# Score matmuls of the first differential attention contract 32 rows instead of 64, and take the maps in another order

## What is computed

```python
def _L2_attn_ref(x, w_qkv, wo, lambda_q1, ..., norm_w):
    b, s, e, H, HD = 4, 512, 128, 16, 8
    q, k, v = to_heads(split(x @ w_qkv, 3))            # 16 heads of 8 dims
    q1, q2 = split(q, 2, axis=-1); k1, k2 = split(k, 2, axis=-1)   # 4 dims each
    a1 = softmax(einsum('bhsd,bhtd->bhst', q1, k1) * HD ** -0.5)
    a2 = softmax(einsum('bhsd,bhtd->bhst', q2, k2) * HD ** -0.5)
    a = a1 - lam * a2
    out = einsum('bhst,bhtd->bhsd', a, v)
    return (out / rms(out) * norm_w * 0.2) ... @ wo
```

## Time and profile before

| | us |
|---|---|
| median of three runs | 1867.42 |
| lowest and highest | 1865.07 and 1871.61 |
| the profiled execution's own time | 1868.42 |
| its span, first to last instruction | 1866.6 |
| the changed stage, kind 2, in the span | about 888 to 1294 |

### The profile page before, as it was taken

How to read it: one execution, slowest core, us unless ns; L and a number is a source line. 1 busy time by engine, 2 the same in 40 slices (tenths; PEclk the granted TensorE clock), 3 DMA queues, 4 the chain that set the end, 5 groups by cost and what they waited for, 6 DMA issues and landing times. The chain is left out here.

```text
span 1866.6 us, 27462 instructions
## 1 busy us (share of the span) xinstructions
PE 1517.4 (81%) x9043; PEld 824.1 (44%) x9102; DVE 1049.9 (56%) x2293; ACT 935.4 (50%) x2171; POOL 364.2 (20%) x507
## 2 busy tenths in 40 slices
PE   4895757999999686675599999997488795999879
PEld 4454643555555475674222222223378452223255
DVE  6577331333334525213788889895511576888656
ACT  3454334444444334112388788875222334888733
POOL 1230630000000162563130101000266101101000
PEclk7796877999999797788699999998698797999979
DMA  2002534020200444543330303000444304223000
GB/s 75 5 1 79 158 112 117 8 68 1 68 1 1 131 127 143 172 127 109 88 80 1 80 1 98 1 1 1 129 139 128 99 1 108 74 66 78 1 1 23
DMA packets 95893, 125.97 MB, mean 67 GB/s; under 512 B 14304, under 2 KB 65120, under 8 KB 95376
## 3 DMA queue, kind: packets, MB, share of 16 engines
q1 hardware_dynamic: 86096, 105.10, 19.7%
q0 software_dynamic: 7936, 16.27, 3.1%
q10 hardware_dynamic: 1728, 2.88, 0.8%
HBM read 87.41 MB, written 36.80 MB: 67 GB/s over the span
## 5 line engine op out<-in xcount | busy, mean ns | idle before, releaser
L2156 DVE TENSOR_REDUCE MAXI<-psum 128x2 f32<-128x1024 f32 x384 | 451.4, 1218 | 70.4 <-PE psum L1962 69.1
L2073 ACT ACTIVATE EX<-psum 128x512 f32<-128x512 f32 x768 | 408.2, 607 | 94.1 <-PE psum L1983 93.6
L2457 PE MATMUL psum<-EX,N 128*128 128x512 f32 x512 | 238.5, 609 | 0.0
L2519 ACT ACTIVATE EX<-psum 128x512 f32<-128x512 f32 x256 | 149.1, 599 | 174.2 <-PE psum L2449 174.2
L1983 PE MATMUL psum<-QM,KM 64*128 64x512 bf16 x768 | 219.8, 389 | 14.7 <-DVE REST L2147 5.0
L1962 PE MATMUL psum<-KM,QS 64*128 64x512 bf16 x768 | 175.1, 405 | 47.7 <-DVE MAXI L2156 22.6
L1993 PE MATMUL psum<-EX,VST 128*32 128x512 f32 x1536 | 205.4, 610 | 1.3 <-ACT OT L2087 1.3
L1191 PE MATMUL psum<-m_DOWN,m_H 128*128 x992 | 143.6, 292 | 35.5 <-DVE m_Y L1416 32.9
L1416 DVE TENSOR_SCALAR m_Y<-psum 128x128 f32<-128x128 f32 x124 | 35.8, 289 | 238.1 <-remote 129.3
L1177 PE MATMUL psum<-m_XT,m_W 128*128 128x128 f32 x992 | 151.9, 302 | 3.4 <-issue 3.4
L2570 DVE COPY OT<-psum 128x512 f32<-128x512 f32 x64 | 44.3, 692 | 187.0 <-PE psum L2457 187.0
(11 more groups left out here) (330 smaller groups left out, 2023.5 us busy)
## 6 DMA issues: line engine op xcount, KB each, us to landing
m_W<-in_w_dram SPq DMA_DIRECT2D x124, 256.0 KB
parts<-PART SPq DMA_DIRECT2D x24, 384.0 KB, 2.6
m_DOWN<-in_w_dram SPq DMA_DIRECT2D x32, 256.0 KB
parts<-PART SPq DMA_DIRECT2D x24, 256.0 KB, 2.5
rows<-N SPq DMA_DIRECT2D x16, 256.0 KB, 3.1
N<-y SPq DMA_DIRECT2D x16, 256.0 KB, 4.1
QS<-parts SPq DMA_DIRECT2D x32, 128.0 KB, 3.8
QS<-parts SPq DMA_DIRECT2D x16, 256.0 KB, 6.0
```

Source lines behind the costliest of these rows:

```text
L2073: act.activation(EX[:, n % 2, kt, MAPS[j], :], bank_of(("score", n, i)), ACT.Exp, scale=SM_SCALE).then_inc(S["exp"].sem, 1)
L2156: dve.tensor_reduce(MAXI[:, n % 2, qt, columns], pair(i), AX, ALU.max, negate=True).then_inc(S["reduced"].sem, 1)
L2457: last = pe.matmul(banks[4 + j], N[:, n // per_b * TB + kt, :], EX[:, n % 2, kt, j, :], start=kt == 0, stop=kt == TB - 1)
L2519: act.activation(EX[:, n % 2, kt, j, :], bank_of(("score", n, i)), ACT.Exp, scale=SM_SCALE, accum_out=SUMS[:, n % 2, j, kt:kt + 1]).then_i ...
```

## The change

A map's peak and score matmuls contract its own 32 partitions. `where` returns `slot * width` to `(slot + 1) * width`; `KM` loses its second copy and with it the clearing of 4 slots by VectorE and 4 by GpSimd and two semaphore waits of TensorE. The scores of kind 2 take the maps in the order 1, 3, 0, 2 (`SCORED`); the peak pairs keep theirs. Kind 3 has slots of 64 partitions and computes as it did. The diff, without the lines that only drop the copy's index from `where`'s result:

```diff
-        half_slots = slots // 2
-        KM = sb("KM", [P, buffers, 8, half_slots, L], BF16)
+        KM = sb("KM", [P, buffers, 8, L], BF16)
...
             slot = j % slots
-            rows = slice(slot // half_slots * 64, slot // half_slots * 64 + 64)
-            return rows, b % buffers, g * stacks + j // slots, slot % half_slots
+            return slice(slot * width, (slot + 1) * width), b % buffers, g * stacks + j // slots
 
         MAPS = {2: (0, 2, 1, 3), 3: (0, 1, 2, 3)}[kind]
+        SCORED = {2: (1, 3, 0, 2), 3: (0, 1, 2, 3)}[kind]
...
-                    if kind == 2 and i == 0 and n == 0:
-                        pe.wait_ge(zeroed.sem, zeroed.at(slots))
-                    if kind == 2 and i == 0 and n == per_b:
-                        pe.wait_ge(filled.sem, filled.at(2 + slots))
...
-                    r, buf, g, m = where(n, MAPS[at])
-                    pe.matmul(bank_of(("score", n, i)), KM[r, buf, g, m, kt * P:(kt + 1) * P],
-                              QM[r, n % 2, MAPS[at] // slots, :], start=True, stop=True).then_inc(S["score"].sem, 1)
+                    r, buf, g = where(n, SCORED[at])
+                    pe.matmul(bank_of(("score", n, i)), KM[r, buf, g, kt * P:(kt + 1) * P],
+                              QM[r, n % 2, SCORED[at] // slots, :], start=True, stop=True).then_inc(S["score"].sem, 1)
...
-                    act.activation(EX[:, n % 2, kt, MAPS[j], :], bank_of(("score", n, i)), ACT.Exp,
+                    act.activation(EX[:, n % 2, kt, SCORED[j], :], bank_of(("score", n, i)), ACT.Exp,
                                    scale=SM_SCALE).then_inc(S["exp"].sem, 1)
...
-                    for j in range(slots):
-                        dve.memset(KM[j * width:(j + 1) * width, 0, :, 1 - j % half_slots, :], 0.0
-                                   ).then_inc(zeroed.sem, 1)
...
-                    if kind == 2 and n < slots:
-                        pool.wait_ge(S["vstage"].sem, S["vstage"].at(n + 1))
-                        pool.memset(KM[n * width:(n + 1) * width, 1, :, 1 - n % half_slots, :], 0.0
-                                    ).then_inc(filled.sem, 1)
-                        pool.wait_ge(filled.sem, filled.at(3 + n))
```

More of the change, by code:

```diff
@@ L1823, in diff_attention @@
         filled = self.semaphore_of("da_filled")
-        zeroed = self.semaphore_of("da_zeroed")
         fixed = self.fixed
@@ L1919, in _ @@
                             to = slice(j * width, (j + 1) * width)
-                            for s, dst in ((0, QS[to, b % buffers, half, :]), (1, KM[to, b % buffers, half, j % half_slots, :])):
+                            for s, dst in ((0, QS[to, b % buffers, half, :]), (1, KM[to, b % buffers, half, :])):
                                 src = scratch[s, b].rearrange("c (d k g) t -> k (c d) g t", k=slots, g=8)[j, :, half, :]
@@ L1960, in peak @@
                     for k in range(2):
-                        r, buf, g, m = where(n, MAPS[2 * jp + k])
-                        last = pe.matmul(pair(i)[:, k, :], QS[r, buf, g, qt * P:(qt + 1) * P], KM[r, buf, g, m, :],
+                        r, buf, g = where(n, MAPS[2 * jp + k])
+                        last = pe.matmul(pair(i)[:, k, :], QS[r, buf, g, qt * P:(qt + 1) * P], KM[r, buf, g, :],
                                          start=True, stop=True)
@@ L1969, in place @@
                     out = bank_of(("place", n, s))
-                    _, buf, g, _ = where(n, s * slots)
+                    _, buf, g = where(n, s * slots)
                     pe.matmul(out, self.identb[:], QS[:, buf, g, :], start=True, stop=False)
@@ L2116, in _ @@
                         src = scratch[1, 0].rearrange("c (d k g) t -> k (c d) g t", k=slots, g=8)[j, :, half, :]
-                        act.dma_start(KM[to, 0, half, j % half_slots, :], src).then_inc(stacked[h].sem, 16)
+                        act.dma_start(KM[to, 0, half, :], src).then_inc(stacked[h].sem, 16)
                 for s in range(stacks):
@@ L2326, in diff_attention @@
         filled.passed(2)
-        if kind == 2:
-            zeroed.passed(slots)
-            filled.passed(slots)
         fixed.passed(32 * B)
```

## The result

| | before | changed |
|---|---|---|
| median of 5 runs, us | 1867.42 | 1884.03 |
| lowest and highest | 1864.67 to 1871.61 | 1878.03 to 1885.69 |
| the profiled execution's own time | 1868.42 | 1885.69 |
| mean granted clock of its span | 0.89 | 0.87 |

The ratio is 1.0083, with a 95% interval of 1.007 to 1.0096. The changed kernel is slower by 0.8%, 16.6 us, where 8.1 us less was forecast.

What follows compares the result with a forecast made beforehand. The stage was taken as bound by a loop through VectorE, ScalarE and TensorE, none full. Savings of 7.2 and 0.9, 8.1 us, took the profiled 1868.42 to 1860.3, or 1859.3 against the median; range 1850 to 1868.

Steps and rivals of the forecast that it cites:

- What bounds the stage, and which steps are on the path: Changed stage: a loop through VectorE, ScalarE and TensorE, none full; two items would go from 21.87 to 21.27 us.
- score 14: TensorE's score matmul behind peak pairs 2 and 3: would start 0.22 us after pair 2, not 0.66.
- pair 6: TensorE's peak pair 6, set by VectorE's reduces: would stay 3.98 us after pair 2.
- pair 0: TensorE's peak pair 0, set by VectorE's chain: would stay about 6.2 us after pair 2.
- the item without a gather: Item of the changed stage that lacks the gather: would save 0.38 us, from 10.47 to 10.09.
- The sum of the gain: Whole kernel: 12 pairs of items at 0.60 us, 7.2, plus 0.9 at changes of batch, 8.1 us saved.
- The 0.3 us for a change of batch: Items at the three changes of batch: half a pair's saving, 0.3 us each, 0.9 together; bounds 0 and 0.6 each.
- The clearing at nothing: Four memsets dropped from VectorE and four from GpSimd: 0 us saved, since both engines then wait anyway.
- The start: Clock's rise at the stage's start: may come later, costing 0 to 3.5 us; 0.5 gained and 0.5 lost taken.
- The clock after the start: Changed stage after the rise: the clock, 0.99 with the value chunks and places, was taken to hold.
- the slower case: Rival: narrower matmuls keep the clock low, 4.7 us per low item; four such items give 10.7 slower, 1878; chance 0.08.
- The rival of a turn worth a part: TensorE's side-by-side matmuls: a saved turn brings 0.15 us instead of 0.22, 5.4 saved, 1862.0; chance 0.10.

Runs made afterwards that it cites:

- the kernel with 14: Kernel before with the new score order; peak pairs 1, 2, 3, 6 and scores 4, 10 to 14 contract their own 32 partitions: 0.9963, again 0.9961.

## Why the prediction was wrong

- **What bounds the stage, and which steps are on the path: right.** Four matmuls of 32 partitions run side by side; score 14, pair 6 and pair 0 stand where they were placed; the item without a gather takes 10.12 (forecast 10.09) and the one with it 11.00 (11.18), since the gather too came 0.18 nearer to pair 0; two items 21.12 (21.27).
- **The sum of the gain: right.** 8.1 us were forecast; the kernel with 14, which has the same steps at the high clock, has a stage 9.8 us shorter, and 8.4 and 8.2 us between the medians on the two chips. The 0.3 us for a change of batch can't be told from this: the long item there takes 14.2 us after the change and 14.1 before.
- **The clearing at nothing: right.** The first maxima of the stage are taken at 920.30, at 920.05 before.
- **The start: the sign was right, the size too small.** The clock rose at 946.1 instead of 935.5. Three items from the first maxima take 34.1 us (920.30 to 954.37) instead of 31.2 (920.05 to 951.23), 2.9 us lost on balance, where 0.5 lost and 0.5 gained were forecast. The range given for the loss, 0 to 3.5, holds it.
- **The clock after the start: the step that failed.** The prediction took "the value chunks and places are as they were, and the clock held at 0.99 with them" as reason enough to give the slower case 0.08. The rows that it stood on the earlier trace rows could show that the clock held with matmuls of 64 partitions; they could not show that the ones of 32 would do. The runs showed nine falls of the clock in the changed stage instead of two, about 95 us at the low level instead of 21, and a loss of 25.4 us against the same steps with the clock held, which turns 8.1 us less into 16.6 more. That rival was priced well: 4.7 us for an item at the low clock and 10.7 us slower with four of them; 25.4 us are 5.4 such items. Its mechanism, its sign and its order of size were what happened.
- **The rival of a turn worth a part: didn't come.** A saved turn was worth the whole 0.22 us. The Trainium skill's 3.07 times for four row tiles ("TensorE: Matmul & The Clock Gate", "Part 3: Packing small matmuls — row/col tiling") isn't what this trace shows from turn to turn: score 12 begins 0.01 us after pair 2 and the next turn 0.22 after that.

What the rows of before could have told: the stage spent 12 us at the low clock with TensorE 95% busy, almost all of it peaks and scores. This was written down as evidence for the rival, and then outweighed by a sentence that was no measurement. It was a hint and no more: with the order alone, and the same 64 partitions, the clock rose 8 us earlier.

## What to carry to other kernels

Matmuls that contract few partitions run side by side on TensorE and save their queueing time, but here a stage full of them lost the high clock for about 95 us instead of 21; where TensorE isn't full, narrow only those that stand on the path and let the others contract their cleared partitions. Keep narrow and wide ones in blocks, since each change between 64 and 32 partitions costs 0.10 us. Before a change that makes a stage's matmuls narrower or fewer, look up the granted clock of the stage. Here it had a mean of 0.97, with two short falls and a late rise; whether these tell beforehand that it has little to spare is an argument from one case. Best here was the kernel with 14 own-partition matmuls of 32, at 0.9963 and 0.9961 of the kernel before.

## What the hardware showed

- Contracting partitions that hold zeros kept the clock up. Before the change half of the 64 contracted partitions were cleared, and the clock of the stage was 0.97; without them it was 0.87, and 0.86 in the old order. Whether it is the partitions or the tiling that goes with them isn't separated.
- Two added matmuls of 128 partitions to an item made the changed kernel 0.9% faster (1.0083 to 0.9996 of the kernel before), with the stage's clock at 0.94 where it had been 0.87, on another chip. The same two with 32 partitions gave 1.0067 and 0.92.
- A change between matmuls of 64 and of 32 partitions takes 0.32 us from start to start, against 0.22 for two that queue in the same partitions.
- A matmul whose partitions are free starts ahead of an older one that waits for its own: one of pair 3's starts with score 12, 0.22 us before its mate, before the change and after.
